# Causal mask of the self-attention layer: second pair of banks added in place by DVE instead of by TensorE products

## What is computed

```python
def _L0_attn_ref(x):
    qkv = x.reshape(B, S, H, hd).transpose(0, 2, 1, 3)
    q = k = v = qkv
    w = jnp.einsum('bhqd,bhkd->bhqk', q, k) / jnp.sqrt(jnp.asarray(hd, x.dtype))
    causal = jnp.tril(jnp.ones((S, S), dtype=bool))
    w = jnp.where(causal[None, None, :, :], w, mask_value)
    w = jax.nn.softmax(w, axis=-1)
    return jnp.einsum('bhqk,bhkd->bhqd', w, v)...
...
x = x + _L0_attn_ref(_layernorm(x, axis=-1))
x = x + _L0_xattn_ref(_layernorm(x, axis=-1), ctx_1024, bias, ...)
x = x + _L0_ffn_ref(_layernorm(x, axis=-1), ...)
```

## Time and profile before

| what | value |
|---|---|
| median of three runs | 434.69 us (434.45 to 435.02) |
| profiled execution, its own time | 432.82 us |
| span of the profile, first to last instruction | 431.1 us |
| PE busy | 318.9 us, 74% |
| DVE busy | 231.1 us, 54% |
| ACT busy | 195.8 us, 45% |
| POOL busy | 253.7 us, 59% |
| mean granted TensorE clock | 0.917 |

### The profile page before, as it was taken

The page is one execution under the profiler, slowest core; times in us unless marked ns, Lnnn a source line. Parts: engine busy times, 40 slices in busy tenths (PEclk is TensorE's granted clock), DMA queues, the critical chain, the costliest instruction groups (busy, mean ns, idle before and its releaser), DMA issues.

```text
span 431.1 us, 9927 instructions
## 1 busy us (share of the span) xinstructions
PE 318.9 (74%) x3467; PEld 206.5 (48%) x3467; DVE 231.1 (54%) x576; ACT 195.8 (45%) x390; POOL 253.7 (59%) x365
## 2 busy tenths in 40 slices
PE   1477888977789999979788788988885410099994
PEld 0133333433556666656544344544453200099993
DVE  5003222257999999977356455656622250057773
ACT  3166555652546546543545536456573200045551
POOL 5853433327799999999887538636341127414544
PEclk9999998999999999999899989999999555579998
DMA  6101434300467898621117990000000002323330
GB/s 165 31 2 42 141 106 118 94 17 14 130 174 192 183 211 205 128 33 17 15 21 161 305 271 4 2 2 2 2 2 2 0 15 107 97 51 100 97 100 17
DMA packets 67040, 36.36 MB, mean 84 GB/s; under 512 B 36253, under 2 KB 56864, under 8 KB 66992
## 3 DMA queue, kind: packets, MB, share of 16 engines
q1 hardware_dynamic: 57040, 15.79, 17.2%
q10 hardware_dynamic: 8448, 16.78, 13.7%
q0 software_dynamic: 1504, 3.16, 2.1%
HBM read 28.48 MB, written 7.69 MB: 84 GB/s over the span
## 4 chain that ended last, share of the span: by engine, by line
PE 33%; POOL 24%; issue 13%; DVE 7%; ACT 6%; DMA 1%; ACTq 1%; POOLq 0%; DVEq 0%
PE pair_banks L561 22%; POOL biased L412 11%; PE work_bank L561 4%; POOL routed_rows L544 3%; PE small_bank L561 3%; ACT probs L877 3%; POOL k_lane L389 3%; POOL rstd L379 2%; PE work_bank L564 2%; DVE rowmax L1031 1%; POOL shift L384 1%; PE small_bank L564 1%; POOL x_sb L437 1%; DVE att L1055 1%; DVE rowsum_inv L1049 1%
## 5 line engine op out<-in xcount | busy, mean ns | idle before, releaser
L877 ACT ACTIVATE probs<-pair_banks 128x1024 f32<-128x1024 f32 x96 | 95.0, 1020 | 54.5 <-PE pair_banks L561 33.4
L412 POOL TENSOR_TENSOR biased<-biased,rowmax 128x1024 f32<-128x1024 f32 x32 | 60.5, 1897 | 15.2 <-DVE rowmax L1023 14.8
L561 PE MATMUL work_bank<-probs,vaug 128*32 128x128 f32 x1536 | 52.7, 278 | 2.5 <-ACT hn2T L891 1.5
L561 PEld LDWEIGHTS work_bank<-probs,vaug 128*32 128x32 f32 x1536 | 39.7, 111 | 12.1 <-issue 8.8
L1031 DVE TENSOR_REDUCE rowmax<-pair_banks 128x8 f32<-128x1024 f32 x32 | 38.9, 1215 | 11.0 <-PE pair_banks L561 10.9
L1049 DVE RECIPROCAL rowsum_inv<-small_bank 128x16 f32<-128x16 f32 x48 | 12.1, 252 | 59.8 <-PE small_bank L564 59.8
L373 POOL TENSOR_SCALAR vareps<-meanvar 128x2 f32<-128x2 f32 x32 | 7.4, 232 | 61.9 <-DVE meanvar L993 60.9
L1016 DVE TENSOR_TENSOR biased<-pair_banks,bias_in 128x1024 f32<-128x1024 f32 x32 | 38.8, 1213 | 8.2 <-PE pair_banks L561 5.1
L561 PE MATMUL pair_banks<-k_lane,qT 32*128 32x512 f32 x256 | 38.6, 675 | 4.3 <-DVE biased L1016 3.9
L551 POOL DMA_INDIRECT out<-vaug x23 | 22.6, 984 | 32.2 <-DVE vaug L1218 20.4
L847 ACT ACTIVATE xn<-x_sb,shift,rstd 128x128 f32<-128x128 f32 x48 | 21.1, 490 | 43.9 <-POOL shift L384 43.9
(11 more groups left out here) (141 smaller groups left out, 570.2 us busy)
## 6 DMA issues: line engine op xcount, KB each, us to landing
bias_in<-in_w SPq DMA_DIRECT2D x16, 256.0 KB, 7.5
routed_rows<-filler SPq DMA_DIRECT2D x2, 1028.0 KB, 9.3
vaug<-routed_rows SPq DMA_DIRECT2D x23, 64.5 KB
biased<-routed_rows SPq DMA_DIRECT2D x23, 64.0 KB
ctx_in<-in_ctx SPq DMA_DIRECT2D x8, 128.0 KB, 4.5
att_scratch<-att SPq DMA_DIRECT2D x16, 64.0 KB, 4.8
att_rows<-att_scratch SPq DMA_DIRECT2D x16, 64.0 KB, 3.5
routed_rows<-filler SPq DMA_DIRECT2D x1, 899.5 KB, 11.9
```

The costliest lines, as they stand in the source:

```text
L412: nc.gpsimd.tensor_tensor(v, v, rowmax[:, b % 2, 8 * half:8 * half + 8].unsqueeze(2).to_broadcast([128, 8, S]), ALU.subtract).then_inc(s_s ...
L561: return nc.tensor.matmul(o, lhsT, rhs, start=start, stop=stop, **kw)
L877: nc.scalar.activation(probs[:, b % 2, 2 * half:2 * half + 2, :], pair("exp", b, half), ACT.Exp, scale=1.0 if layer(b) == CROSS else SCALE ...
```

## The change

In the self layer PE masks the first half only. In the second half the first of the score products starts the accumulation, and DVE then adds `causal` to the two banks in place, in PSUM, in one instruction of 128 by 1024 elements (`mask_second_half`). The exponentials of the second half wait for that (`s_masked`) instead of for the products. The claim of the second pair of banks moves from before the third mask to before the score products of both halves.

```diff
                 for g in range(NG):
...
-                                   start=start, stop=kind == "max" or layer(b) == SELF, tile_position=(G * HD * g, 0)))
+                                   start=g >= 2 if start is None else start, stop=kind == "max" or layer(b) == SELF, tile_position=(G * HD * g, 0)))
...
             def self_scores(b):
-                for g in range(NG):
-                    if g % 2 == 0:
-                        claim(PAIR_BANKS["exp", b, g // 2])
+                claim(PAIR_BANKS["exp", b, 0])
+                for g in range(2):
                     mm(bank_of("exp", b, g), identb[:], causal[:].rearrange("p g k -> p (g k)"), stop=False)
+                claim(PAIR_BANKS["exp", b, 1])
                 pe.wait_ge(s_qlane, b // 2 + 1)
-                done = row_products("exp", b, kT, q_lane, start=False)
+                done = row_products("exp", b, kT, q_lane, start=None)
...
             def exponentials(b, half):
-                act.wait_ge(s_e, 2 * b + half + 1)
+                if layer(b) == SELF and half == 1:
+                    act.wait_ge(s_masked, b + 1)
+                else:
+                    act.wait_ge(s_e, 2 * b + half + 1)
...
+            def mask_second_half(b):
+                dve.wait_ge(s_ident, 5)
+                dve.wait_ge(s_e, 2 * b + 2)
+                banks = pair("exp", b, 1)
+                nc.vector.tensor_tensor(banks, banks, causal[:].rearrange("p g k -> p (g k)").unsqueeze(1).to_broadcast(
+                    [128, 2, G * S]), ALU.add).then_inc(s_masked, 1)
...
                     row_maxes(b + 2, 0, FIRST_STEP)
+                if b < FIRST_CROSS:
+                    mask_second_half(b)
                 if 0 <= b - 2 < NB:
                     attention(b - 2)
```

More of the change, by code:

```diff
@@ L210, in build @@
         s_e = sem("scores_ready")
+        s_masked = sem("second_half_masked")
         s_p = sem("probs_ready")
```

## The result

The changed kernel takes 440.27 us (median of four runs, 437.58 to 442.06) against 434.57 us for the kernel before (median of four runs): 1.0125 times the time, 95% interval 1.0063 to 1.0187. A second comparison, with eight runs of the changed kernel, gave 437.85 against 434.05 us, 1.0084 times (1.0046 to 1.0122). Forecast were 439.0 us. The profiled execution has a span of 440.2 us and took 442.06 us; it is the slowest of the four, and the profiled execution of the kernel before, 432.82 us, was faster than its median, so the rows of the two overstate the median difference.

The account below looks back on a forecast made before the run. A two-slot loop from PE over DVE, POOL and ACT back to PE was taken to bound the self layer; 1.5 + 0.5 - 1.1 + 0.4 + 3.0 = +4.3 us on 434.69 gave 439.0 us, range 435.0 to 441.8.

Parts of the forecast that it names:

- The addition: DVE adding the mask to the second half in place in PSUM: 1.2 us, taken from the bias addition's 1.215 us.
- Its place: Addition ahead of the attention on DVE lengthens the loops of slots 3, 5, 7, 9 by 0.37 us each: +1.5 us.
- The claim: PE waits for the second half's bank ahead of all products: cost nothing, a stall if ACT were a microsecond later.
- Slot 1: Addition ahead of pair 4's statistics starts POOL 1.0 us and ACT 0.7 us later, before slot 3's transposes: +0.5 us.
- Slots 11 to 13: Chain through both slots' products: fewer masks save time, later second halves and normalisation take over half back: -0.6 us.
- Slot 7: If the clock is low there again, two masks fewer save 0.94 instead of 0.48 us: -0.5 us.
- Slots 14 and 15: First row maxima on DVE come about 0.06 us later in slot 14, a further 0.34 in slot 15: +0.4 us.
- The clock: Longer gaps ahead of odd slots lower PE's clock to 0.50 in slots 3, 5, 9 too: 1.0 us each, +3.0 us.
- the clock didn't hold: Rival that the clock holds: gaps grow but it falls no more often than now; +1.3 us, 436.0 us, chance 0.2.
- the addition was not cheap: Rival of a cheap, hidden mask: addition 0.86 us, loops unchanged; -1.0 us, 433.7 if the clock holds, chance 0.12.
- The bound by PE's own work: Rival that PE's work is the bound: 32 masks of 0.24 us fall away, 7.7 us, 427.0 us, chance 0.03.
- The price of a doubled addition: Rival that the addition costs double, 2.43 us: loops and other slots grow further, 448 us or so, chance 0.05.

Follow-up runs that it names:

- filled gaps: Overwritten products added on PE in the gap ahead of odd slots 3 to 11: eight in the changed kernel (433.62 us), four in the kernel before (431.61 us).

## Why the prediction was right

By the medians, the forecast of +4.3 us stands between the two measured differences, 5.7 and 3.8 us. The split into two causes holds as well. The forecast had 2.4 us for the place (1.5 + 0.5 + 0.4) and 1.9 us for the clock (3.0 for new falls, less 1.1 where masks are saved at the slow clock). With filled gaps the place measures 2.2 us; the falls measure 4.2 us in the changed kernel and 2.0 in the kernel before, a difference of 2.2. Each of these has an interval of a microsecond or more, so that they agree to tenths is luck.

The traces are less kind to the sizes. The table takes the self layer apart at the transposes ahead of each odd slot and at POOL's first subtraction of block 17. It gives how much longer each part takes than in the profile before (33.51, 42.65, 51.79, 62.56, 71.69, 83.38 and 104.28 us), in the first profile of the changed kernel (34.17, 45.11, 56.16, 67.39, 77.50, 88.52 and 111.11 us) and in the one of the second comparison (34.12, 45.24, 56.46, 66.05, 77.26, 88.28 and 110.88 us).

| part | forecast us | first profile | second profile |
|---|---|---|---|
| up to slot 3 | +0.5 | +0.66 | +0.61 |
| slots 3 and 4 | +1.37 | +1.80 | +1.98 |
| slots 5 and 6 | +1.37 | +1.91 | +2.08 |
| slots 7 and 8 | -0.13 | +0.46 | -1.18 |
| slots 9 and 10 | +1.37 | +0.98 | +2.08 |
| slots 11 and 12 | -0.6 | -0.67 | -0.67 |
| slots 13 to 15 | +0.4 | +1.69 | +1.70 |
| sum | +4.3 | +6.83 | +6.60 |

The forecast of a loop is 0.37 us, with 1.0 us more for a new fall (slots 3, 5 and 9) and 0.5 us less where masks are saved at the slow clock (slot 7). In the traces the self layer loses 2.3 to 2.5 us more than forecast: a full fall costs more than 1.0 us, and slot 15 more than 0.34. That the medians come out nearer to the forecast than this is in part luck. The profiled execution before took 1.75 us less than its median, and the part behind the subtraction scatters by more than these differences (last section).

- **What bounds the kernel**: right. The loop from PE over DVE, POOL and ACT back to PE carries the self layer. PE's idle gaps, not its 74%, decided: eight useless products in each of them helped the changed kernel and cost it nothing.
- **The addition**: 1.2 us forecast, 1.233 us measured. Reading and writing the same banks in place is hardly dearer than the bias addition (1.215 us). The Trainium skill, page VectorE: DVE Perf Modes, section "The perf-mode tier table (the rule you actually need)", has `tensor_tensor` with an operand in PSUM at the plain rate; the trace agrees, as the bf16 operand made the addition no faster.
- **Its place**: 0.37 us for each loop forecast, 9.60 - 9.13 = 0.47 measured. The mis-sized piece is the start: DVE begins 55.50 - 53.40 = 2.10 us after the transposes, not 1.96, as the addition waits for the end of all products, 0.16 us behind their last record.
- **The claim**: no cost forecast. In slots 3 to 13 PE's rows show no idle time between the two masks and the products.
- **Slot 1**: +0.5 forecast; the transposes ahead of slot 3 come at 34.17 instead of 33.51 us, +0.66.
- **Slots 11 to 13**: -0.6 forecast. From the transposes ahead of slot 11 to those ahead of slot 13 it is 11.02 instead of 11.69 us, -0.67. This saving belongs to the slow clock: with filled gaps, at full clock, it is 10.33 against 10.23 us.
- **Slot 7**: -0.5 forecast for masks saved at the slow clock, which the runs don't show. When the clock fell there again, the loop grew by 0.46 us, as much as at full clock. The fall then began earlier: the transposes took 0.69 instead of 0.45 us and the products 2.09 instead of 1.92.
- **Slots 14 and 15**: 0.06 and 0.34 us forecast. By the first profile of the changed kernel with filled gaps and the one of the kernel before with filled gaps, at full clock in both, block 17's subtraction is at 104.57 against 101.63, 2.94 us, while the transposes ahead of slot 11 are at 72.60 against 70.51, 2.09. So 0.85 us arise behind slot 11, 0.75 of them in slots 13 to 15, about twice the forecast; without filled gaps it is 1.7 us, as the clock fell in slot 15 in both profiles of the changed kernel.

```profile
104.57 1.90 POOL L414 TENSOR_TENSOR biased<-biased,rowmax 128x1024 f32<-128x1024 f32 x1 [2.97 <-DVE rowmax L1032]
```

```profile
101.63 1.90 POOL L413 TENSOR_TENSOR biased<-biased,rowmax 128x1024 f32<-128x1024 f32 x1 [2.62 <-DVE rowmax L1028]
```

- **The clock**: the mechanism was right, its size was not quite. Three new falls at 1.0 us were forecast, and slots 3, 5 and 9 had them in the profile. A loop with a full fall takes 10.94 to 11.23 us against 9.60, 1.3 to 1.6 us, while the fall of slot 9 came late and cost 0.5. An additional fall in slot 15 (1.03 us for two masks at 105.11 us) was not forecast. Work put into the gap brought 2.4 GHz back. The Trainium skill, page TensorE: Matmul & The Clock Gate, section "What's actually happening", says that activity releases the throttle; the runs with filled gaps agree.
- **The rivals**: the clock didn't hold; the addition was not cheap. The bound by PE's own work is spoken against by the gaps, which grew. The price of a doubled addition was set too low, at 448 us: doubled it gives 459.28. Of the 18.2 us by which its subtraction of block 17 comes later than that of the changed kernel, 11.3 arise behind the transposes ahead of slot 11. There it stands on the chain in each of slots 11 to 13 (88.52, 95.19 and 101.39 us) and not once in two, and the clock fell in slot 14 too (2.09 us for its products). The same reading hid how much two masks fewer are worth there.

## What to carry to other kernels

Before work is moved off the busiest engine, look for its idle gap and for who ends it: here four masks stood behind the wait that ends the gap, and moving them ahead of it took 0.70 us out of each loop and gave 1.6% without a new instruction. An operation on an idle engine is not free if what closes the loop is queued behind it. And taking work off TensorE widens its gaps and can cost clock: here the falls took 2.2 us more after the change.

## Unexpected on the hardware

Products whose results are overwritten shortened a kernel: 4.2 us in the changed kernel and 2.0 us in the kernel before, by holding the granted clock at 1.00 and 0.99 from 28 to 97 us. Over the profiles of all runs, in slots 5 to 11, it never fell behind gaps of 0.56 to 1.67 us, fell behind some of those of 1.79 to 2.50 us, and behind all of those of 2.85 to 3.38 us. The length of the last gap alone does not decide: without the addition the clock fell in slot 7 behind 2.41 us and held in slot 5 behind the same 2.41 us. What else decides is not shown.

The part behind the self layer is less steady than the runs before the change let me think: from POOL's first subtraction of block 17 to the end it takes 326.8 us in the profile of before (431.1 - 104.28), 329.1 in the one after (440.2 - 111.11) and 323.5 in the one with the gap filled (428.1 - 104.57), with the same code there. The kernel before itself ran between 430.73 and 436.63 us in 29 runs on one chip, so a few tenths of a per cent need many runs here. No run tries what makes that part scatter.
